# A graph network with product-key memory: edges counted for 32 destinations at a time, and x multiplied by the weights before the aggregation

## The chip, the cores and the metric

The kernel runs on one core of one Trainium2 chip. The metric is the device time of one execution in microseconds (us), the median of several runs.

## The reference, cut to what matters

x is 1250 x 512, float32. The graph has 21,250 edges (10,000 random pairs in both directions and 1250 loops), sorted by destination. Four stages follow each other, each added to x:

```python
x = x + L0_gnn(layernorm(x))    # the stage that the change touches
x = x + L0_ffn(layernorm(x))    # 8 heads, top 8 of 256 x 256 keys, two 512-wide rows gathered for each hit
x = x + L1_gnn(layernorm(x))    # aggregation over the same edges
x = x + L1_ffn(layernorm(x))    # one of 8 experts for each row
```

Stage L0_gnn, written out:

```python
xw = x @ W.T
row, col = concat(src, loop), concat(dst, loop)
dinv = rsqrt(segment_sum(1, col))
out = segment_sum(dinv[row] * dinv[col] * xw[row], col) + b
h = (out - mean(out)) * rsqrt(var(out) + eps) * gamma + beta   # mean, var over the 1250 rows
return gelu(h) + x
```

## The kernel before

The rows are padded to 1280, which is NT = 10 tiles of 128. The core first builds the dense table of edge counts AT[source, destination] (1280 x 1280, float32) and uses it for both aggregations.

Counting (`pe_program`, L1573 to L1602; `act_program`, L679 to L710; `dve_program`, L986 to L1029). The edge list is loaded as NS = 84 rows of 256 edges and transposed, so that 128 edges lie on the partitions. For each tile t of 128 destinations the registers hold which edge rows touch it (`pairs_of`, L645: one load from SBUF and two register results), and a loop runs over them. A step takes four blocks of 128 edges. VectorE writes for each block a 128 x 1280 fp16 table of marks (L996) that says which source each edge has; ScalarE writes a 128 x 128 fp16 table that says which destination (L681, L689); TensorE multiplies the two and adds up in PSUM (L1580, 1280 columns for a block). ScalarE copies a finished tile of counts to AT (`keep_counts`, L695). Between tiles VectorE adds up columns (L1008, L1010), TensorE finishes the sums (L1570, in-degrees), and VectorE takes the row statistics of x (L933).

Aggregation. VectorE makes the degree roots and scaled rows h0 (L1045 to L1055), and TensorE multiplies h0 with AT (`piece`, L1608: 4 feature blocks, 10 source tiles, three ranges of 512, 512 and 226 destinations). VectorE scales by the destinations' roots (L1086) and TensorE multiplies with the weights (L1657: 4 output blocks, 4 feature blocks, the same three ranges). Beside it one reduction over all of AT gives the out-degrees (L1073), the residual is formed (L1080), loops are taken off AT (L1093), and ScalarE turns AT into int16 for the second graph stage (L740).

Batch norm and gelu, for each block o of 128 features (`out_row` and `gelu`, L744 to L760, and L1107 to L1117): ScalarE adds the bias, VectorE takes statistics, ScalarE a square root, VectorE the scale and shift, ScalarE the gelu. Square root and gelu need different activation tables, each with its own load.

Then comes the memory stage (L763 on): searches, indirect gathers of 2 x 512 numbers by GpSimd (L587, each 128 rows), dot products on VectorE (L1313), a diagonal on ScalarE (L883) and a product on TensorE (L1786). It begins with the first tile whose four feature blocks have had their gelu. The last stages are L1714, L1861 and L1883.

The order on each engine is the order of the program; each engine waits for counters of the others. SP issues the loads in this order: edges, x, first weights, parameters, query weights, keys, and 34 writes that clear a scratch table in HBM.

## Time and profile before

| what | value |
|---|---|
| runs | 1264.42, 1264.74, 1264.78 us; median 1264.74 |
| profiled execution, first to last instruction (span) | 1262.0 us; 2.7 us lie around it when set against the median of the runs |
| TensorE, VectorE, ScalarE, GpSimd busy | 91%, 73%, 41%, 51% of the span |
| counting | 14.9 to 134 us |
| aggregation | 134 to 222 us |
| product with the first weights | 222 to 256 us |
| memory stage | from 260 us; first gather issued at 284.9 us |

The profile names engines PE (TensorE), PEld (its weight loads), DVE (VectorE), ACT (ScalarE), POOL (GpSimd) and SP; a q behind a name is the engine's sequencer, which does register work, waits and branches. A float32 matmul shows as two records.

### The profile page before, as it was taken

How to read it: one execution, taken by the hardware profiler on the slowest of the kernel's cores; microseconds unless marked ns; L12 is line 12 of the kernel's file. 1: busy time of each engine (PE TensorE's matmuls, PEld its weight loads, DVE VectorE, ACT ScalarE, POOL GpSimd, SP SyncE). 2: the span in 40 equal slices, each digit the busy share in tenths (PEclk: the TensorE clock that was granted, in tenths of full speed). 3: DMA queues.
4: the chain of work that ended last, by engine and by line, in shares of the span. 5: the costliest groups of instructions: out<-in, count | busy, mean ns of one | idle time of the engine just before them, and what ended most of it. 6: DMA issues, size and time to landing. Idle time of an engine off the chain costs nothing.

```text
span 1262.0 us, 15214 instructions
## 1 busy us (share of the span) xinstructions
PE 1145.0 (91%) x3900; PEld 572.9 (45%) x3901; DVE 925.5 (73%) x2783; ACT 514.7 (41%) x1254; POOL 640.5 (51%) x698
## 2 busy tenths in 40 slices
PE   5999999965999998899998998989989889989497
PEld 2555555553444444354444444534444344334243
DVE  6999831357899987978879789788797877665311
ACT  7889103642435343443444434443444333320010
POOL 1000000007667777777777776777767776631322
PEclk9999999986999999999999999999999999989699
DMA  8999000008989999999999999999999999944643
GB/s 336 418 421 418 29 0 1 1 0 345 383 353 388 409 409 408 409 409 410 409 409 408 410 409 408 409 410 408 409 409 397 410 408 381 410 174 163 234 139 109
DMA packets 107763, 406.07 MB, mean 322 GB/s; under 512 B 11946, under 2 KB 12112, under 8 KB 103332
## 3 DMA queue, kind: packets, MB, share of 16 engines
q0 software_dynamic: 92992, 337.10, 67.6%
q1 hardware_dynamic: 14692, 68.07, 13.8%
q8 instruction: 30, 0.49, 0.2%
q14 instruction: 49, 0.40, 0.1%
HBM read 353.24 MB, written 53.00 MB: 322 GB/s over the span
## 4 chain that ended last, share of the span: by engine, by line
PE 53%; DVE 14%; DMA 13%; POOL 9%; issue 5%; ACT 2%; DVEq 2%; ACTq 0%; SPq 0%; POOLq 0%
PE tr L1786 19%; PE acc L1580 8%; DMA big<-in_wdu,idx 7%; PE acc L1608 7%; POOL big L587 6%; PE acc L1714 4%; DMA AT<-in_wdu,idx 4%; DVE big L1313 4%; PE acc L1687 3%; PE tr L1883 3%; PE acc L1657 3%; POOL AT L587 3%; PE tr L1861 2%; PE acc L1698 2%; DVE AT L1313 2%
## 5 line engine op out<-in xcount | busy, mean ns | idle before, releaser
L587 POOL DMA_INDIRECT big<-in_wdu,idx x460 | 434.2, 944 | 435.3 <-DVE idx L1377 279.3
L1786 PE MATMUL tr<-big,diag 128*128 128x512 f32 x920 | 427.1, 602 | 31.8 <-ACT diag L883 31.2
L1313 DVE CUSTOM_DVE_ANT_0 big<-big,acc,prob 128x512 f32<-128x512 f32 x460 | 322.9, 742 | 68.2 <-DMA big<-in_wdu,idx 66.7
L883 ACT ACTIVATE diag<-ident,inner 128x128 f32<-128x128 f32 x576 | 199.3, 393 | 414.2 <-DVE inner L1313 412.3
L1786 PEld LDWEIGHTS tr<-big,diag 128*128 128x128 f32 x920 | 166.9, 190 | 249.0 <-issue 167.1
L587 POOL DMA_INDIRECT AT<-in_wdu,idx x168 | 163.6, 974 | 61.8 <-issue 46.0
L1786 PE MATMUL tr<-AT,diag 128*128 128x512 f32 x336 | 157.0, 600 | 8.7 <-ACT diag L883 8.7
L1313 DVE CUSTOM_DVE_ANT_0 AT<-AT,acc,prob 128x512 f32<-128x512 f32 x168 | 118.0, 743 | 25.2 <-DMA AT<-in_wdu,idx 24.2
L1580 PE MATMUL acc<-outT,diag 128*128 128x512 f16 (+1 forms) x600 | 112.7, 349 | 4.0 <-ACT diag L689 3.8
L996 DVE TENSOR_SCALAR outT<-big 128x1280 f16<-128x1280 f16 x200 | 96.6, 547 | 6.1 <-PE acc L1580 3.2
L1786 PEld LDWEIGHTS tr<-AT,diag 128*128 128x128 f32 x336 | 61.0, 190 | 86.2 <-issue 62.1
L1687 PEld LDWEIGHTS acc<-yT,qk 128*128 128x128 f32 x640 | 79.9, 199 | 18.7 <-issue 16.6
L1608 PE MATMUL acc<-AT,big 128*128 128x512 f32 (+1 forms) x240 | 84.6, 513 | 0.0
L1580 PEld LDWEIGHTS acc<-outT,diag 128*128 128x128 f16 x600 | 59.1, 100 | 54.5 <-ACT diag L689 3.5
L1687 PE MATMUL acc<-yT,qk 128*128 128x128 f32 x640 | 82.5, 284 | 1.4 <-ACT yT L777 1.4
L1714 PE MATMUL acc<-wide,h1bc 128*128 128x512 f32 (+1 forms) x144 | 60.9, 518 | 3.6 <-issue 3.6
L1608 PEld LDWEIGHTS acc<-AT,big 128*128 128x128 f32 x240 | 45.4, 190 | 37.9 <-issue 37.8
L681 ACT ACTIVATE gt<-big 128x128 f16<-128x128 f16 x200 | 61.4, 387 | 2.1 <-issue 2.0
L1313 DVE DVE_READ_ACCUMULATOR2_ANT inner<- 128x1 f32 x628 | 51.8, 82 | 0.0
L1698 PE MATMUL acc<-qk,qT 64*128 64x256 f32 x288 | 50.6, 428 | 0.0
L1714 PE MATMUL acc<-wide,gt 128*128 128x512 f32 (+1 forms) x96 | 43.7, 551 | 6.3 <-ACT wide L830 4.3
L1173 DVE TENSOR_TENSOR outT<-outT,acc 128x512 f32<-128x512 f32 (+1 forms) x60 | 35.0, 585 | 16.8 <-PE acc L1714 16.7
(301 smaller groups left out, 1068.7 us busy)
## 6 DMA issues: line engine op xcount, KB each, us to landing
sorted_rows<-big SPq DMA_DIRECT2D x33, 1280.0 KB, 32.7
big<-in_we SPq DMA_DIRECT2D x8, 1024.0 KB, 14.6
big<-in_wdu,idx POOLq DMA_INDIRECT x460, 10.6
x<-sorted_rows SPq DMA_DIRECT2D x14, 512.5 KB, 3.5
AT<-in_wdu,idx POOLq DMA_INDIRECT x168, 10.8
x<-in_x SPq DMA_DIRECT2D x1, 2304.0 KB
qk<-in_wq SPq DMA_DIRECT2D x1, 2048.0 KB, 15.4
big<-in_w0t SPq DMA_DIRECT2D x1, 1024.0 KB, 12.3
```

The lines of the kernel that those rows point to most:

```text
L587: pool.indirect_dma_start(out=k.slot[r * GS + s], out_offset=None, in_=k.wdu_d, in_offset=bass.IndirectOffsetOnAxis(ap=k.idx[i % 2][:, j:j ...
L681: ins = act.activation(k.far[:, (half * BPS + b) * P:(half * BPS + b + 1) * P], k.iota[:, NPAD + t * P:NPAD + (t + 1) * P], ACT.Abs, bias= ...
L883: ins = act.activation(k.diag[:, c * P:(c + 1) * P], to, ACT.Relu, scale=k.inner[:, j:j + 1])
L996: ins = dve.tensor_scalar(k.ohs[:, (half * BPS + c) * NPAD:(half * BPS + c + 1) * NPAD], k.iota[:, t * P:t * P + NPAD], k.key[:, bass.ds(c ...
L1313: ins = dve.tensor_tensor_reduce(out=row, in0=row, in1=k.Y[i % 2] if i < NT - 1 else k.Yh[j // WIDTH], scale=k.prob[:, (i % 2) * HK + j:(i ...
L1580: ins = pe.matmul(acc[:, c0:c0 + n], k.ohb[:, (half * BPS + b) * P:(half * BPS + b + 1) * P], k.ohs[:, (half * BPS + b) * NPAD + c0:(half ...
L1608: return pe.matmul(k.acc[s][:, c0:c0 + n], k.h0[:, t * D + f * P:t * D + (f + 1) * P], k.AT[:, t * NPAD + c0:t * NPAD + c0 + n], start=(t ...
L1657: ins = pe.matmul(k.acc[o % 2][:, c0:c0 + n], k.w0[:, f * D + o * P:f * D + (o + 1) * P], k.aggT[:, f * NPAD + c0:f * NPAD + c0 + n], star ...
L1687: ins = pe.matmul(k.Q[:, (h % 4) * P:(h % 4 + 1) * P], k.wq[:, f * H * P + h * P:f * H * P + (h + 1) * P], k.yT[:, f * P:(f + 1) * P], sta ...
L1698: ins = pe.matmul(k.S[:, c, 0:NK], k.qT[half, (h % 4) * P:(h % 4 + 1) * P], k.keys[half, h * NK:(h + 1) * NK], start=True, stop=True)
L1714: ins = pe.matmul(k.G[n % 2 if n >= TWO_BANKS else 0][:, 0:cols], k.h1[j % 3][:, f * P:(f + 1) * P], k.wide[:, at:at + cols], start=(j == ...
L1786: ins = pe.matmul(k.O[i % 2], k.diag[:, c:c + P], row, start=(g == 0 and s == 0), stop=(g == groups_of(i) - 1 and s == GS - 1))
```

## The change

The change replaces the stage L0_gnn and its preparation:

- Counting goes by windows of WIN = 32 destinations, NW = 40 in all. An edge block's stationary operand is a 128 x 128 fp16 table: source modulo 128. The moving operand is 320 marks: 10 source tiles times 32 destinations. The stationary tables of all 168 blocks are made once, before the loop, by `one_hots`; the marks are made in the windows by `marks`. Each window takes FIXED = 2 edge rows in straight code, with two sets of buffers, and the rest (at least one) in a loop with one buffer. Columns are chosen by a register.
- In-degrees come from a histogram of small products before the windows (destination modulo 32 times destination divided by 32), not from sums over AT.
- TensorE multiplies x, loaded once more in transposed form, by the first weights before the aggregation. The layer norm's mean is taken out of the weights (W less its mean over the features, by GpSimd), and its scale goes onto the product (`keep_xw`).
- The aggregation multiplies the result with AT, by range of destinations: 12 parts, of which eight run between windows (`PART_AFTER`) and four, of 226 destinations, after the last. VectorE scales a part, ScalarE adds the bias.
- The diagonal of roots, the loops in AT and the int16 table go to GpSimd. The out-degree reduction stands in two halves around the first of the last four parts, ahead of the batch norm of block 0; the residual lies between the batch norms.
- SP loads w0 and x transposed ahead of x, clears the scratch table in 68 writes, and loads query weights and keys after the last window.

```diff
-SPAN = BPS // 2 * P
+SPAN = 2 * P
+WIN = 32
+NW = NPAD // WIN
+CODES = NT * WIN
+FIXED = 2
+PARTS = [(c0, n, o) for c0, n in SPANS for o in range(FT)]
+PART_AFTER = {17: 0, 20: 1, 23: 2, 26: 3, 33: 4, 35: 5, 37: 6, 39: 7}
+TILES_OF = [4, 8, NT]
 def pool_program(pool, k):
...
+    pool.wait_ge(k.wmean_ready, 1)
+    for f in range(FT):
+        rows = k.w0[:, f * D:(f + 1) * D]
+        pool.tensor_tensor(rows, rows, k.wmean, ALU.subtract)
+    pool.drain().then_inc(k.wc_ready, 1)
...
+    for t in range(NT):
+        pool.wait_ge(k.at_done, (t + 1) * (P // WIN))
+        pool.tensor_tensor(loops(t), loops(t), k.ident[:, :], ALU.add).then_inc(k.loops_done, 1)
+    pool.wait_ge(k.sums_done, 1)
+    for t in range(NT):
...
+        pool.tensor_tensor(loops(t), loops(t), k.ident[:, :], ALU.subtract)
+        pool.drain()
+        pool.tensor_copy(k.few[:, t * NPAD:(t + 1) * NPAD] if t else k.few0, k.AT[:, t * NPAD:(t + 1) * NPAD])
 def act_program(act, k):
...
+    keep_xw(0)
+    for w in range(NW + 2):
+        if w < NW:
+            keep_counts(w)
+        for t in kept_after.get(w, []):
+            keep_xw(t)
...
+        if w - 2 in PART_AFTER:
+            biased(PART_AFTER[w - 2])
 def dve_program(dve, k):
...
+    def one_hots(out, codes, n, block):
+        cols = slice(block * BLOCK, (block + 1) * BLOCK)
+        return dve.tensor_tensor(out[:, 0:n, cols], codes[:, cols].unsqueeze(1).to_broadcast([P, n, BLOCK]),
+                                 k.iotaX[:, 0:n, :], ALU.is_equal)
+    for block in range(4):
+        one_hots(k.lo_hot, k.lo16, WIN, block)
+        one_hots(k.hi_hot, k.hi16, NW, block)
+        dve.drain().then_inc(k.hist_ready, 1)
...
+    for block in range(4):
+        one_hots(k.table, k.src16, P, block)
...
+    def marks(w, first):
+        end, shift = rows_of(dve, k, w)
+        base = column(dve, k, (first + shift) * 2, 2 * (NS - 1))
+        for row in range(FIXED):
+            if w >= 2 and row == 0:
+                dve.wait_ge(k.fixed_used, w - 1)
+            for c in range(2):
+                ins = dve.tensor_scalar(k.fixed[w % 2][2 * row + c], k.iota,
+                                        k.key[:, 2 * row + c:KEYS][:, bass.ds(base, 1)], -float(CODES * w),
+                                        ALU.subtract, ALU.is_equal)
+            ins.then_inc(k.fixed_ready, 1)
+        with dve.Fori(first, end) as row:
+            col = column(dve, k, (row + shift) * 2, 2 * (NS - 1))
+            dve.wait_ge(k.looped_used, row + 1)
...
+            ins.then_inc(k.looped_ready, 1)
+    first = marks(0, 0)
+    dve.wait_ge(k.indeg_psum, 1)
...
+        stats(k.x[:, t * D:(t + 1) * D], t)
...
+    first = marks(1, first)
...
+    dve.drain().then_inc(k.coef_ready, 1)
+    for w in range(2, NW + 4):
+        if w < NW:
+            first = marks(w, first)
+        if w - 2 in PART_AFTER:
+            scaled_part(PART_AFTER[w - 2])
+        if w - 4 in PART_AFTER:
+            part_stats(PART_AFTER[w - 4])
...
+    out_degrees(0, NT // 2)
+    scaled_part(EARLY)
+    out_degrees(NT // 2, NT)
+    dve.drain().then_inc(k.sums_done, 1)
...
+    norm_row(0)
+    scaled_part(EARLY + 1)
+    for t in range(NT // 2):
+        residual(t)
+    norm_row(1)
+    scaled_part(EARLY + 2)
+    for t in range(NT // 2, NT):
+        residual(t)
...
+    norm_row(2)
+    scaled_part(EARLY + 3)
+    norm_row(3)
 def pe_program(pe, k):
...
+    def window(w, first):
+        end, shift = rows_of(pe, k, w)
+        base = column(pe, k, (first + shift) * 2, 2 * (NS - 1))
+        if w >= 2:
+            pe.wait_ge(k.at_done, w - 1)
+        for row in range(FIXED):
+            pe.wait_ge(k.fixed_ready, FIXED * w + row + 1)
+            for c in range(2):
+                ins = chunk(w, base, 2 * row + c, k.fixed[w % 2][2 * row + c], row == 0 and c == 0)
+        ins.then_inc(k.fixed_used, 1)
+        with pe.Fori(first, end) as row:
...
+            pe.wait_ge(k.looped_ready, row + 1)
+            for c in range(2):
+                ins = chunk(w, col, 2 * FIXED + c, k.looped[c], False)
+            ins.then_inc(k.looped_used, 1)
...
+    weighted(0)
+    pe.wait_ge(k.bounds_ready, 1)
...
+    histogram()
+    weighted(1)
+    weighted(2)
+    in_degrees()
+    weighted(3)
+    pe.wait_ge(k.table_ready, 1)
+    first = 0
+    for w in range(NW):
+        first = window(w, first)
+        if w + 4 < NT:
+            weighted(w + 4)
...
+        if w in PART_AFTER:
+            part(PART_AFTER[w])
+    for p in range(EARLY, len(PARTS)):
+        part(p)
```

## Rows read from the trace of the kernel before

**Rows 1.** The page: its span and the busy time of each engine.

```profile
span 1262.0 us, 15214 instructions
PE 1145.0 (91%) x3900; PEld 572.9 (45%) x3901; DVE 925.5 (73%) x2783; ACT 514.7 (41%) x1254; POOL 640.5 (51%) x698
```

**Rows 2.** Busy time in stretches: PE, PEld, DVE, ACT, POOL, clock, DMA share, GB/s.

```profile
30.00:110.00 80.00, 79.58 (x475) 45.01 (x473) 77.52 (x158) 71.30 (x180) 0.00 (x0) 1.00 1.01 419
160.00:210.00 50.00, 50.00 (x144) 27.17 (x143) 11.22 (x20) 4.02 (x4) 0.00 (x0) 1.00 0.00 0
300.00:1100.00 800.00, 750.39 (x2368) 360.67 (x2369) 664.90 (x2138) 331.01 (x869) 585.62 (x617) 0.99 1.02 403
```

**Rows 3.** The chain that ended last, in order of time: start, length, what.

```profile
4.37 0.42 DVE big L937
14.89 13.77 PE acc L1580 x60
51.77 10.84 PE acc L1580 x60
159.47 62.95 PE acc L1608 x180
222.42 33.21 PE acc L1657 x94
259.60 2.01 ACT outT L756 x3
```

**Rows 4.** The first gather, in the timeline of GpSimd.

```profile
284.88 1.21 POOL L587 DMA_INDIRECT big<-in_wdu,idx  x1 [279.28 <-DVE idx L1377]
```

**Rows 5.** Groups by shape, 0 to 262 us: shapes and count, busy, mean ns, idle before.

```profile
L681 ACT ACTIVATE gt<-big 128x128 f16<-128x128 f16 x200 | 61.4, 387 | 2.1 <-issue 2.0
L1073 DVE TENSOR_REDUCE degin<-AT 128x10 f32<-128x12800 f32 x1 | 13.5, 13487 | 0.1
L933 DVE BATCH_NORM_STATS2 st<-x 128x6 f32<-128x512 f32 x10 | 6.8, 685 | 0.0
L1080 DVE TENSOR_SCALAR x<-x,pq 128x512 f32<-128x512 f32 x10 | 4.7, 545 | 0.1
L747 ACT ACTIVATE outT<-acc,par 128x226 f32<-128x226 f32 x4 | 1.8, 443 | 0.0
```

**Rows 6.** The same list, by shape, 262 to 1262 us, and of GpSimd.

```profile
L1224 DVE TENSOR_TENSOR pick<-pick,topf 128x1024 f16<-128x1024 f16 x9 | 6.2, 692 | 0.8
L607 POOL TENSOR_TENSOR x<-x,qk 128x512 f32<-128x512 f32 x10 | 12.3, 1279 | 0.3 <-issue 0.3
```

**Rows 7.** VectorE's timeline in the counting: start, length, what.

```profile
13.11 3.79 DVE L996 TENSOR_SCALAR outT<-big 128x1280 f16<-128x1280 f16 x8 [1.36 <-issue]
```

**Rows 8.** The sequencers' records at L647, L996 and L1022: ns min/median/max.

```profile
L647 DVEq TENSOR_LOAD <-bnd x10: 306/570/646, 11.9 to 107.6; - x10
L647 DVEq FUSED_REGOPS  x10: 190/211/212, 12.5 to 108.2; - x10
L996 DVEq FUSED_REGOPS  x200: 57/57/202, 13.0 to 129.8; - x100
L1022 DVEq COMPARE_BRANCH  x20: 50/56/80, 19.8 to 130.1; - x20
```

**Rows 9.** Small matmuls in the timeline, 118 to 162 us.

```profile
120.14 0.23 PEld L1602 LDWEIGHTS acc<-big 128*128 128x128 f16 x3
```

**Rows 10.** The end of the stage before, in the timeline of 222 to 262 us.

```profile
239.91 1.28 ACT L750 ACT_TABLE_LOAD   x1
241.20 0.29 ACT L750 ACTIVATE bsd<-bmv,eps 128x1 f32<-128x1 f32 x1
241.51 1.28 ACT L756 ACT_TABLE_LOAD   x1
242.81 1.46 ACT L756 ACTIVATE outT<-outT,bsc 128x1280 f32<-128x1280 f32 x1
```

**Rows 11.** Busy time in stretches, as in rows 2: in the start of the memory stage.

```profile
290.00:300.00 10.00, 2.52 (x12) 1.79 (x11) 8.00 (x32) 1.54 (x2) 7.72 (x8) 0.50 0.97 364
```

718 lines of the change are left out of this document (326 added, 392 removed).

## The prediction

> **What bounds the kernel now.** Read the page's busy times first, then stretches, then the chain of waits. TensorE is busy 91% of the span [rows 1], but for different reasons: while it counts and aggregates it never rests (79.6 of 80 us, 50.0 of 50, [rows 2]); in the memory stage (300 to 1100 us) it is busy too, but there the DMA share is 1.02 at 403 GB/s, and the change touches neither. The chain is one TensorE line after another until the last product with the weights ends at 255.6 us, and the batch norm's last block starts its gelu at 259.6 [rows 3]; the first gather follows at 284.9 [rows 4]. So the question is only when that gelu starts; everything later moves with it, one for one. The profiled execution spans 1262.0 us and the median of the runs is 1264.7, so I work out differences and take them from 1264.7.
>
> **What TensorE saves.** Before, 60 matmuls of the counting, which are 20 blocks of 1280 columns in three pieces each, take 10.84 us [rows 3]: 0.54 us a block, 0.42 ns a column. I ran the reference's input formula for the graph: with rows of 256 edges the 40 windows touch 2 to 4 rows each, and with 2 fixed and at least 1 looped row they run 124 rows, 248 blocks (four windows, 11, 19, 25 and 31, loop twice). At 320 columns that is 248 x 320 x 0.42 = 33.6 us, 0.14 a block, 0.85 a window with one loop; before it was 119 us. The float32 products stay: 180 records in 62.95 us [rows 3] are 90 matmuls, 30 each of 512, 512 and 226 columns, 1.68 ns a column, so 0.86 us for 512 columns. A tile of x times weights is 4 of these, 3.44 us, ten are 34.4 (before 33.2); a part of 512 destinations is 10, 8.6 us, eight are 69; a part of 226 is 3.8, four are 15. New: a histogram of 168 pairs (weight load, product). Three fp16 pairs of one column take 0.23 us [rows 9], so 0.075 each and 12.6 us; half and double that (6 to 25) are its ends. TensorE alone would be some 55 us shorter. What follows says how much of it waits.
>
> **Before the windows.** VectorE starts at 4.4 as before [rows 3]. Codes, flags and bounds are ops of 0.4 us like L937's; I take 10 us for the start of the one-hots. An fp16 tensor_tensor of 1024 elements takes 0.69 us [rows 6]: 0.53 for elements at two a cycle, 0.16 fixed. A histogram block (1408 and 1760 elements) is 2.0 us, four 8.0; bounds 1.7; four table blocks of 5632 elements 3.1 each, 12.3: done at 32. (At one element a cycle the blocks would be done at 50, and the windows 5 later.) TensorE: flips until 11, four sums over w0 3.4, ScalarE's mean 0.7, four subtractions on GpSimd at 1.23 (ten of them in 12.3, [rows 6]) to 20.3, tile 0 to 23.9, histogram to 36.6, tiles 1 and 2 to 43.5, in-degrees to 44.5, tile 3: window 0 begins at 48. Its end is at 49, but then tile 4 needs a bank freed by `keep_xw`, which waits for coef_ready. That chain is on VectorE: degrees 0.5 after 44.5, ten statistics of x 6.2 to 6.9 [rows 5], their aggregation 0.9, marks of window 1 (2.3, below), roots 0.8, ScalarE's copy 0.7: 56. TensorE idles 7 us behind it; everything in its queue, tiles and windows, is behind that wait.
>
> **Windows.** VectorE's mark op of 1280 fp16 elements repeats every 0.474 us (8 in 3.79, [rows 7]): four elements a cycle leave 0.33, so 0.14 is fixed and 320 elements cost 0.22. Six are 1.3 us. The sequencer needs more: the load of the window's word 0.31 to 0.57, two register results 0.21, the base column about 0.2, 0.06 for each mark's address, branches 0.06 each [rows 8]; with 0.07 to issue an op that is 2.2. Before, this work hid behind marks of 0.47; now the loop's wait for `looped_used` lets little overlap. I take 2.3 us a window where VectorE sets the pace; ends 1.7 (all register work hidden but one load) and 3.2 (nothing overlaps, and the round trip to TensorE, about 0.7, is added). Where TensorE has other work VectorE runs up to 1.7 windows ahead and a window costs TensorE its 0.85 to 1.
> - Tiles 4 to 9 beside windows 1 to 5: 6 x 3.44 + 5 x 0.95 = 25.4, from 56 to 81.5, and 1.7 for a slow clock after the idle time: at 25% busy the granted clock was 0.50, 1.2 GHz [rows 11]. 83.
> - Windows 6 to 17: 12 x 2.3 = 27.6, and 1.5 for the spread of roots: 112.
> - Eight parts, 68.8, in which nothing counts. Windows between them: after a part the first costs 0.85, the second 1, the third 2.6 with the scaling in VectorE's queue (0.7, taken like the statistics of 512 columns, [rows 5]): three triples 13.5; windows 27 to 33 4.5 + 4 x 2.3 = 13.7; three pairs 5.7. Second loops 2.8, slow clock at parts 0 and 4 3.4. Part 7 ends at 112 + 107.9 = 220.
> ScalarE's copies of counts (320 columns; 128 cost 0.39, [rows 5]) take about 0.6 a window and hide. GpSimd's loops and roots hide too: forty windows lie over them. The scratch table's writes are over long before the gathers, at 400 GB/s for 44 MB.
>
> **The tail grows.** Before, the four parts of the last 34 us came 8.3 us apart, and a block's norm (6 us) fitted under the next one's product; only 4 us stood behind TensorE. Now four parts end 3.8 us apart, but the norms queue. After part 7: scaling, bias, statistics 2.4; half of the out-degrees 6.7 (the whole is 13.5 for 12,800 elements, [rows 5]), scaling of part 8 0.5, the other half 6.7: 16.3. Then block 0: statistics, aggregation, root, table load, gelu. One block costs table 1.28, root 0.3, table 1.28, gelu 1.46 [rows 10] and 0.44 of bias; the residual (five of 0.5, L1080 in [rows 5]) stands before the statistics of blocks 1 and 2. Block 0's gelu ends at 20.5, block 1's at 26.4 (its table is loaded by the degree root before it), block 2's at 31.8, and block 3's starts at 35.1. TensorE's own last part ended at 15: 20 us of tail stand open against 4 before.
>
> **Sum.** 220 + 35.1 = 255.1 against 259.6: 4.5 us earlier. GpSimd's int16 copies of AT can start at 16.3 after part 7 and have until the first gather, 25.3 after the gelu, thus 44 us for ten steps and an eleventh copy. A subtraction of 128 columns is about 0.3, the drains 0.4, a copy of 1280 between 1.3 (an element a ns) and 3.1 (L607's 2.4 ns an element): 22 to 42 us. It fits, barely at the upper end. Query weights (3 MB, some 8 us after window 39) land long before. Forecast 1264.7 - 4.5 = 1260.2, say 1260. By its own terms this case holds 1253 to 1266: half the histogram's price is -6, 0.3 on 20 VectorE-bound windows is +6.
>
> **Rivals.**
> A. The windows are cheap: at 1.7 instead of 2.3 us 20 windows give 12 back: 1248. For it: register loads are hidden before (idle before L996 for issue is a single 1.36 at the start, [rows 7]). Against: the ops that hid them were twice as long.
> B, slower. The hand-over between VectorE and TensorE decides: each window has a load on both sequencers and one single looped buffer, so marks, signal, product and signal stand in a row. From 2.55 us a window on it eats the gain (4.5 over 20 windows is 0.22); at 3.1 it costs 16 more: 1276. For it: sequencer work of over 1 us a window is in rows 8. Against: only one row a window uses the single buffer, and the next window's fixed marks can be written meanwhile.
> C, slower. GpSimd's subtraction, which TensorE waits for before tile 0, is held by VectorE's one-hots. If each of the last two of its four operations waits for a table block of 3.1 us, window 0 begins 7 us later: 1267. No row shows the two engines so; ten operations of GpSimd beside VectorE's sums out of PSUM kept 1.23 us [rows 6]. The Trainium skill, SBUF — State Buffer, section "SBUF: two separate sides", says that VectorE (with two SBUF inputs) and a GpSimd operation reading SBUF take a shared port pair exclusively for a whole instruction; by that rule C comes true, and otherwise not.
> D. The marks with two arithmetic steps run at one element a cycle: 0.25 more each, 1.5 a window: 1290.
> E. GpSimd's copies are late and hold the first gather: each us over 4 a copy costs 11; at 4.5, 1266.
>
> **Chances.** Forecast 0.42 (of it faster 0.30, no change 0.08, slower 0.04), A 0.18, B 0.19, C 0.13 (0.02 of it no change), D 0.03, E 0.05 (0.03 no change). A measurement tells about 0.2%, 2.5 us, from no change. Faster: 0.30 + 0.18 = 0.48, and 0.04 more where B and C are partly made good by A: 0.52. No change 0.13, slower 0.35. The range reaches from A's 1248 to most of B: 1247 to 1275; the forecast's own is 1253 to 1266.
>
> **What would show it.** Window 0 at about 48 us, tile 4 at 56; a mark of about 0.2 us; VectorE-bound windows every 2.3 us with TensorE under half busy; part 7 ending near 220; the last gelu's start 35 us behind it. If parts and tail are right and the windows differ, the sum fails in the 2.3. If the tail is under 30 or the gathers don't follow 25 us after the gelu, the chain that I wrote down isn't the one that binds. Forecast is wrong outside 1253 to 1266.

## The result, and the profile after

| what | value |
|---|---|
| kernel before | 1264.76 us median (1264.42 to 1265.6, 4 runs) |
| changed kernel | 1291.96 us median (1291.04 to 1292.48, 4 runs) |
| ratio | 1.0215, 95% interval [1.0200, 1.0229]: slower by 27.2 us |
| predicted | 1260.0 us (1247 to 1275), faster: wrong, and on the wrong side |

The page of the changed kernel, as in [rows 1]:

```profile
span 1289.1 us, 14872 instructions
PE 1121.7 (87%) x3670; PEld 567.4 (44%) x3671; DVE 896.2 (70%) x2788; ACT 420.0 (33%) x1029; POOL 681.9 (53%) x754
```

TensorE, VectorE and ScalarE all do less work than before, and the kernel is slower: the time is idle time and a lower clock, not work. The stretches (columns as in [rows 2]) are windows 6 to 17, the eight parts with windows 18 to 39, and the memory stage:

```profile
96.20:129.50 33.30, 22.13 (x102) 14.21 (x100) 16.20 (x68) 7.22 (x16) 1.39 (x3) 0.59 1.01 404
129.50:245.60 116.10, 102.87 (x324) 52.79 (x323) 40.50 (x149) 14.34 (x30) 2.80 (x6) 0.91 0.08 29
300.00:1100.00 800.00, 739.48 (x2383) 359.42 (x2384) 669.74 (x2179) 327.57 (x856) 580.41 (x607) 0.99 1.00 395
```

In windows 6 to 17 (first line) TensorE is busy 22 of 33 us, and that at a granted clock of 0.59, between its two levels 0.50 (1.2 GHz) and 1.00 (2.4 GHz); VectorE, which I had as the engine that sets the pace, is busy only 16. The memory stage (last line) moves its bytes nearly as before. The chain that ended last, in order of time:

```profile
16.60 6.50 POOLq L618
23.14 5.79 PE acc L1619 x8
29.17 16.92 PE tr L1629 x168
46.09 9.66 PE acc L1619 x16
...
58.43 4.75 DVE st L977 x8
68.19 5.45 PE acc L1619 x8
...
127.71 1.82 PE acc L1642 x6
129.54 10.57 PE acc L1679 x20
...
236.85 8.71 PE acc L1679 x20
247.89 6.68 DVE degout L1115
254.86 6.73 DVE degout L1115
...
284.91 2.01 ACT outT L797 x3
```

From top to bottom: GpSimd's subtractions, tile 0, the histogram, tiles 1 and 2, (cut) VectorE's statistics of x, tile 4, (cut) window 17, part 0, (cut) part 7, the two halves of the out-degrees, and (cut) the gelu of block 3. That gelu began at 259.60 before [rows 3]: it is 25.3 us later, and the kernel 27.2. The first gather follows 26.0 behind it, as it did before (25.3, [rows 4]):

```profile
310.86 1.21 POOL L657 DMA_INDIRECT big<-in_wdu,idx  x1 [27.91 <-DVE idx L1416]
```

So the frame of the prediction held: what counts is when that gelu starts. The four stages before it, each against what the prediction has:

| stage | predicted us | measured us | late by |
|---|---|---|---|
| start, to the end of window 5 | 0 to 83 | 0 to 96.2 | 13.2 |
| windows 6 to 17, and spreading the roots | 29 | 33.3 | 4.3 |
| eight parts and windows 18 to 39 | 107.9 | 116.1 | 8.2 |
| tail, part 7's end to block 3's gelu | 35.1 | 39.3 | 4.2 |

Together 29.9, and 1.9 more come behind the gelu; 1260.2 + 31.8 is the measured time.

### The profile page after: what moved, and what is told of

Read it like the earlier page. It is cut to its first block, busy times and chain, and to the rows that moved or that the text cites. A ratio compares the mean times of both kernels' runs of the same rounds, so it can differ in the third digit from the quotient of the medians.

```text
span 1289.1 us, 14872 instructions
## 1 busy us (share of the span) xinstructions
PE 1121.7 (87%) x3670; PEld 567.4 (44%) x3671; DVE 896.2 (70%) x2788; ACT 420.0 (33%) x1029; POOL 681.9 (53%) x754
## 4 chain that ended last, share of the span: by engine, by line
PE 47%; DVE 18%; DMA 13%; POOL 9%; issue 7%; DVEq 3%; ACT 2%; POOLq 1%; SPq 0%; ACTq 0%
PE tr L1835 18%; DMA big<-in_wdu,idx 7%; PE acc L1679 6%; POOL big L657 6%; DVE big L1352 4%; PE acc L1763 4%; DMA AT<-in_wdu,idx 4%; PE acc L1736 3%; PE acc L1642 3%; POOL AT L657 3%; PE acc L1619 3%; PE tr L1932 3%; PE tr L1910 2%; DVE AT L1352 2%; PE acc L1747 2%
## 5 line engine op out<-in xcount | busy, mean ns | idle before, releaser
L1835 PE MATMUL tr<-big,back 128*128 128x512 f32 x920 | 428.7, 603 | 31.7 <-ACT back L927 30.9
L927 ACT ACTIVATE back<-ident,inner 128x128 f32<-128x128 f32 x576 | 199.3, 394 | 414.2 <-DVE inner L1352 412.3
L1835 PEld LDWEIGHTS tr<-big,back 128*128 128x128 f32 x920 | 167.0, 190 | 250.4 <-issue 167.7
L1835 PE MATMUL tr<-AT,back 128*128 128x512 f32 x336 | 157.0, 600 | 8.0 <-ACT back L927 7.9
L1763 PE MATMUL acc<-front 128*128 128x512 f32 (+1 forms) x240 | 98.8, 532 | 10.4 <-issue 6.0
L1835 PEld LDWEIGHTS tr<-AT,back 128*128 128x128 f32 x336 | 61.1, 190 | 85.4 <-issue 61.6
L1736 PEld LDWEIGHTS acc<-front 128*128 128x128 f32 x640 | 79.9, 199 | 18.7 <-issue 16.6
L1736 PE MATMUL acc<-front 128*128 128x128 f32 x640 | 82.7, 284 | 1.4 <-ACT front L821 1.4
L1065 DVE TENSOR_SCALAR back<-big 128x320 f16<-128x320 f16 x88 | 23.0, 302 | 73.0 <-PE acc L1642 72.5
L1763 PEld LDWEIGHTS acc<-front 128*128 128x128 f32 x240 | 44.5, 194 | 62.0 <-issue 56.9
L1057 DVE TENSOR_SCALAR back<-big 128x320 f16<-128x320 f16 x160 | 38.6, 304 | 33.8 <-issue 26.9
L1222 DVE FIND_INDEX8 topi<-top,back 128x8 uint32<-128x256 f32 x144 | 58.5, 419 | 0.0
```

Of the source, the lines that this page charges most:

```text
L927: ins = act.activation(k.diag[:, c * P:(c + 1) * P], to, ACT.Relu, scale=k.inner[:, j:j + 1])
L1222: ins = dve.max_index(k.topi[:, c * HK + h * 8:c * HK + h * 8 + 8], k.top[:, c * HK + h * 8:c * HK + h * 8 + 8], k.sc[h % 2][:, c * NK:(c ...
L1736: ins = pe.matmul(k.Q[:, (h % 4) * P:(h % 4 + 1) * P], k.wq[:, f * H * P + h * P:f * H * P + (h + 1) * P], k.yT[:, f * P:(f + 1) * P], sta ...
L1763: ins = pe.matmul(k.G[n % 2 if n >= TWO_BANKS else 0][:, 0:cols], k.h1[j % 3][:, f * P:(f + 1) * P], k.wide[:, at:at + cols], start=(j == ...
L1835: ins = pe.matmul(k.O[i % 2], k.diag[:, c:c + P], row, start=(g == 0 and s == 0), stop=(g == groups_of(i) - 1 and s == GS - 1))
```

## Experiments

Where nothing else is said, a kernel is the changed one with only the edit shown. "Gelu" is the start of block 3's gelu in its trace (259.6 before, 284.9 in the changed kernel). The kernel before, run beside each group, took 1264.3 to 1264.9 us, with one exception told at e9.

One thing has to be known for reading "gelu". Tile 0 begins at 23.0 to 23.5 us in some traces (the changed kernel, e6, e9, e10, e12, e13, e16) and at 26.3 in others (e1, e3, e4, e5, e14, e17), though nothing in front of it was edited; why is told at rival C. So gelus of two traces compare within 3 us only. Lengths of single stretches don't have this error.

**e1_stats_early.** The statistics of x before VectorE's wait for the histogram.

```diff
+    (statistics of x and their aggregation)
     dve.wait_ge(k.hist_psum, 1)
...
     dve.drain().then_inc(k.degs_ready, 1)
-    (statistics of x and their aggregation)
```

> The row statistics of x and their aggregation (7.1 us on VectorE from 57 to 64 us, on the way to the scale that tile 4 of x times weights waits for) are moved ahead of the copy of the histogram, where VectorE stood idle for 10.5 us. Theory 1, the preparation sets the start and everything behind it is delayed one for one: tile 4 starts some 6 to 7 us earlier (at about 62 instead of 68.2), the total falls by as much, to about 1285.5. Rival, the windows' own pace absorbs it (the first windows become bound by marks): less than 3 us.

Measured 1286.32 us (1284.14 to 1286.97), ratio 1.0168 [1.0151, 1.0185]: 5.6 less than the changed kernel. Tile 4 began at 65.8 in place of 68.2 although tile 0 began 3.2 later in this trace (26.3, against 23.1): the wait was real. From tile 0 to the end of tile 9 this trace needs 64.9 us, the changed kernel 72.3, 7.4 less, a little more than the 6 to 7 of theory 1. Where the statistics stand is worth 5 us or more.

**e2_hist_first.** TensorE's histogram in the place where it waited for GpSimd.

```diff
-    weighted(0)
+    histogram()
     pe.wait_ge(k.bounds_ready, 1)
...
-    histogram()
+    weighted(0)
     weighted(1)
```

> TensorE's order only: the 168 small products of the histogram stand ahead of tile 0, in the 7.2 us that TensorE idled until GpSimd had taken the mean off the weights. Theory 1: window 0 and tile 4 come about 6 us earlier, total about 1286. Rival, the small products run at the lower clock there and tiles 0 to 3 then too, or the histogram waits for its marks of VectorE until 20.8 us: 2 to 4 us, total about 1289.

Measured 1282.45 us (1280.65 to 1283.73), ratio 1.0141: 9.5 less, more than both theories had. The chain of this kernel has no GpSimd in it any more; the sums over w0 are followed at once by the histogram, and that by three tiles:

```profile
11.06 5.62 PE acc L1608 x8
16.69 16.92 PE tr L1629 x168
...
33.96 13.10 PE acc L1619 x24
```

The histogram keeps its 16.9 us. The granted clock over it is 0.66 here and 0.65 in the changed kernel, although here TensorE was busy without a break before it and in it: the clock fell over these small products without any wait. The idle 7 us before tile 0 are gone, and so is some of the slow clock behind them: tiles 0 to 2 take 13.1 here, 15.5 in the changed kernel (5.79 and 9.66).

**e3_outdeg_split.** The out-degrees range by range between the windows, only the last range in the tail.

```diff
     for w in range(2, NW + 4):
...
+        if w == 22: degrees_of(0)    # 10 x 512 columns
+        if w == 37: degrees_of(1)
...
-    out_degrees(0, NT // 2)
-    scaled_part(EARLY)
-    out_degrees(NT // 2, NT)
+    degrees_of(2)                    # 10 x 256 columns
+    scaled_part(EARLY)
+    (two sums of 128 x 10)
```

> The out-degree reduction (13.5 us in two halves behind part 7, ahead of block 0's batch norm) is done by ranges of destinations: the first 512 and the second 512 in VectorE's idle time beside parts, 256 at the end. Theory 2, the tail is one chain behind part 7 and the reduction stands in it: the 13.5 become 2.7 and two small additions, the last gelu starts 10 us earlier, total about 1282. Rival, the chain of table loads and batch norms behind the last parts (15 us from part 7 to the end of part 11) takes over: part 8 to 11 end 3.8 us apart and a block needs 4.9, so 7 to 8 us, total about 1284.5. If it gave nothing, the tail is not what binds.

Measured 1285.25 us (1283.64 to 1286.07), ratio 1.0162: 6.7 less. The tail itself fell from 39.3 to 27.8 us, more than either theory had; the rest was lost before it. The first of the two stood one or two windows too late in VectorE's order. VectorE's timeline in this kernel:

```profile
157.93 0.52 DVE L1065 TENSOR_SCALAR back<-big 128x320 f16<-128x320 f16 x2 [6.79 <-PE acc L1651]
158.66 5.49 DVE L1109 TENSOR_REDUCE degout<-AT 128x10 f32<-128x5120 f32 x1 [0.22 <-issue]
```

The marks of a looped row wait 6.8 us for TensorE, which is busy with a part; only then does the reduction start, when TensorE needs marks again. Part 2 began 7.3 us later than in the changed kernel (of which part 0 already had 1.9), and so part of the gain was paid back. An operation meant to hide under a part must stand ahead of the marks that wait for that part.

**e4_static.** The rows of each window as constants in the code: no word loaded, no register column, no loop; same buffers, waits and order. It holds for this graph alone.

```diff
-    word = eng.value_load(k.bnd[0:1, w:w + 1], ...)
-    return eng.snap(word >> 12), eng.snap((word & (END - 1)) - SHIFT)
+    first = sum(LOOPED[:w])
+    return first + LOOPED[w], LOWS[w] - first
...
-        with dve.Fori(first, end) as row:
+        for row in range(first, end):
```

> The rows that each window takes are constants of this graph: no register loads, no address work, no loop; the marks, products, buffers and waits are the same. Theory 3, register work on VectorE's and TensorE's sequencers sets the pace (theory of the prediction, 2.3 us a window of which 1.3 is marks): windows 8 to 17 fall from 2.6 us to about 1.5, the total by about 20, to 1272. Rival, the hand-over over the single buffer of the looped row (signal, marks 0.5, signal, two products, signal): windows stay above 2.2 us and the total falls by less than 8. Second rival, TensorE at 1.2 GHz sets it (six products take 1.82 us instead of 0.83): windows stay at about 2.2.

Measured 1263.22 us (1259.73 to 1265.45, 10 runs), ratio 0.9983 [0.9972, 0.9994]: 28.7 less, as much as the whole loss against the kernel before (27.2). That doesn't make it the only thing that costs: e1, e2 and e3 find their gains elsewhere. The clock is full from 100 us to the end of part 7,

```profile
100.00:120.00 20.00, 17.14 (x91) 10.32 (x90) 15.53 (x68) 6.07 (x14) 1.58 (x3) 1.00 1.02 406
120.00:160.00 40.00, 36.79 (x128) 18.92 (x128) 16.56 (x64) 5.78 (x12) 1.08 (x2) 1.00 0.26 103
```

and windows that nothing else disturbs come 1.27 us apart, which is VectorE's six marks.

**e5_fill.** Is the clock the cause or the consequence? Two fp16 products of 512 columns that nothing reads, behind each of windows 9 to 33 that no part follows.

```diff
+        if 8 < w < 34 and w not in PART_AFTER:
+            for _ in range(2):
+                pe.matmul(k.tr[1], k.zero[:, 0:P], (512 columns), start=True, stop=True)
```

> Two products of 512 fp16 columns that nothing reads stand behind each window from 9 to 33 that has no part behind it; they take TensorE 0.43 us at 2.4 GHz, 0.86 at 1.2. Everything else is the changed kernel. Theory, the low clock (granted 0.50 from 100 to 120 us) sets the pace of the windows: the clock stays at 2.4 GHz, windows fall from 2.6 to about 2.1 us, parts 0, 2 and 4 lose their slow start (1.8 us each), the total falls by 10 or more, to about 1281. Rival, register work sets it and the low clock is only what follows from TensorE's waiting: the clock rises but windows stay at 2.4 to 2.6, and only the slow starts go: 3 to 6 us, total about 1287. If the filler stands in the way, the total rises.

Measured 1287.07 us (1284.7 to 1288.57), ratio 1.0168: 4.9 less.

```profile
120.00:160.00 40.00, 34.37 (x126) 17.54 (x124) 15.97 (x63) 5.60 (x12) 0.99 (x2) 0.96 0.27 105
```

```profile
122.12 1.25 PE L1642 MATMUL acc<-back,front 128*128 128x320 f16 x6 [0.79 <-ACT AT L752]
...
123.32 0.59 PE L1664 MATMUL tr<-front,big 128*128 128x512 f16 x2
124.77 1.22 PE L1642 MATMUL acc<-back,front 128*128 128x320 f16 x6 [0.85 <-ACT AT L752]
```

The first row is the stretch, the others TensorE's timeline; the third is the two added products. The granted clock is up (0.96, against 0.83 over 120 to 160 us in the changed kernel; 1.00 over 118 to 124, against 0.50 over 118 to 123), and the windows still come 2.6 us apart, with 0.8 us in which TensorE does nothing. One might object that the added products eat what the clock gives (0.59 us here, and six products took 1.82 and now 1.22). The records of TensorE's sequencer rule that out. The load of the window's word starts at 120.7 and 123.3 here, while the added products still run, and at 118.5 and 121.1 in the changed kernel: 2.6 us both times, 1.4 from the load to the first of the six products and 1.2 to issue the six. The low clock does not make the pace, the sequencer does. The parts gained, since fewer of them start slow: part 0 takes 8.8 us, 10.6 in the changed kernel.

**e6_ahead.** Each window's word is loaded one window ahead, before the loop, on both engines.

```diff
     def marks(w, first, rows):
         end, shift = rows
...
+        if w + 1 < NW:
+            rows = rows_of(dve, k, w + 1)
         with dve.Fori(first, end) as row:
```

> The general kernel with its loops, but each window's word is loaded and taken apart (0.31 + 0.20 us on VectorE's sequencer, 0.31 + 0.16 on TensorE's) before the loop of the window in front, where the sequencers wait for each other anyway. Theory, the register work stands on the chain of the window (the 28.7 us that the constants gave back are mostly loads and results of loads): 0.5 us a window in 14 windows bound by it, 6 to 10 us in all, total about 1284. Rival, it is the loop itself (its column register, the two branches, the end) that the constants took away: under 3 us.

Measured 1292.61 us (1291.72 to 1293.43): no gain. The latency of the load is not what is waited for. The records of the sequencers say why: they work one instruction after another, and the load takes its time of a sequencer wherever it stands (VectorE's and TensorE's in the changed kernel, ns min/median/max):

```profile
L717 DVEq TENSOR_LOAD <-big x40: 299/312/820, 46.4 to 227.1; - x40
L717 DVEq FUSED_REGOPS  x40: 190/204/205, 47.3 to 227.5; - x40
...
L1057 DVEq FUSED_REGOPS  x160: 57/64/202, 47.7 to 228.5; - x160
...
L1061 DVEq COMPARE_BRANCH  x44: 43/43/67, 49.3 to 235.8; - x44
...
L717 PEldq TENSOR_LOAD <-big x40: 295/306/771, 55.7 to 229.7; - x40
L717 PEldq FUSED_REGOPS  x40: 156/157/165, 56.5 to 230.1; - x40
...
L1642 PEldq FUSED_REGOPS  x248: 46/52/146, 57.0 to 236.3; - x124
```

All such records of a window, summed with the medians, are 1.29 us on VectorE and 1.10 on TensorE. The medians hide two levels of the load. Here are the loads of the changed kernel from 98 to 127 us, then from 131 to 245:

```profile
L717 PEldq TENSOR_LOAD <-big x10: 489/556/630, 100.5 to 126.4; - x10
L717 DVEq TENSOR_LOAD <-big x9: 546/569/586, 99.5 to 124.9; - x9
```

```profile
L717 PEldq TENSOR_LOAD <-big x22: 295/300/308, 131.3 to 229.7; - x22
L717 DVEq TENSOR_LOAD <-big x20: 299/304/315, 142.9 to 227.1; - x20
```

Up to 127 us the writes of the scratch table run (408 GB/s over 100 to 127); behind them a load takes half as long. The step lies at 126 to 131 us in e5, e12, e13 and e17 too, whichever window is due then. No run moved the writes, so that they are the reason is argued, not shown. In windows 6 to 17 the sums are thus about 1.55 us on VectorE and 1.35 on TensorE.

**e9, e10, e14: load and columns, or loop?** In e9 the loops' lengths are constants and the loops straight code; the word is loaded and every column is a register. In e10 the loops stay, with constants for their ends and for the first row; the looped row's column comes out of a register only where a loop runs twice (the trace shows 8 column results in place of 88).

```diff
 e9:
-    return eng.snap(word >> 12), eng.snap((word & (END - 1)) - SHIFT)
+    return sum(LOOPED[:w + 1]), eng.snap((word & (END - 1)) - SHIFT)
-        with dve.Fori(first, end) as row:
+        for row in range(first, end):
 e10:
-    word = eng.value_load(...)
-    return eng.snap(word >> 12), eng.snap((word & (END - 1)) - SHIFT)
+    first = sum(LOOPED[:w])
+    return first + LOOPED[w], LOWS[w] - first
         with dve.Fori(first, end) as row:
```

> The changed kernel, but each window's number of looped rows stands in the code, so the step that was in a loop is straight code; each window's word is still loaded into a register on both engines, and every column still comes from a register. Constants for everything gave 28.7 us back, loading the word a window ahead gave nothing. Theory: the loop itself (its branch, the register work and waits inside it that nothing can be moved past) makes a window 2.6 us; then this run keeps at least 20 of the 28.7 us: 1265 to 1272, windows 6 to 17 at 1.3 to 1.8 us. Rival: the load and the register columns are the cost (six columns computed for each engine in each window), the loop only adds its branch of 0.06 us; then it gains under 8: 1284 to 1291, windows 2.3 us or more.

> The counterpart: loops stay loops (one pass, in four windows two), but their ends, and the columns of the two fixed rows, are constants; no word is loaded; only the looped row's column is computed from the loop's counter. If the loop itself is the cost, this stays near the changed kernel: 1280 to 1290, windows 6 to 17 at 2.2 to 2.6 us. If the load and the fixed rows' register columns are, it comes close to constants for everything: 1264 to 1270. If each has its own share, the two runs lie about half way each, near 1277.

> The kernel with loops and constants once more, on a chip where the kernel before takes 1264 and not 1367 us. In its first trace block 3's gelu began at 253.8 us, 31 earlier than in the changed kernel and 5.8 earlier than before. If the later stages follow one for one, it takes 1259 (1256 to 1262); if loops with constants delay something that only the later stages show, it stays at 1264 to 1267, as the first ratio (1.0019) had it.

These (and e11, e15) ran in two sessions in which every kernel took 100 us longer: the kernel before had 1366.73 and 1369.9 us there. The traces of e9 to e11 move 357 GB/s over 300 to 1100 us, e14's 360, in place of 403; up to the gelu they look like the others. They bear the chip number of e1 to e4, so what differed is not known. e9 took 1379.97, ratio 1.0088 [1.0058, 1.0118]; e10 1369.37, ratio 1.0019 [0.9995, 1.0043]; e14, the same kernel, 1366.85, ratio 1.0003 [0.9978, 1.0028]. The question of e14, and of e15 below, how fast the kernel is where the one before takes 1264 us, stayed open. The changed kernel was not timed in them, so I compare the starts of the gelu: 269.1 in e9, 253.8 and 257.1 in e10 and e14 (tile 0 begins 2.8 us later in e14), 256.2 in e4. VectorE in e10:

```profile
108.49 0.51 DVE L1070 TENSOR_SCALAR back<-big 128x320 f16<-128x320 f16 x2
108.91 0.93 DVE L1062 TENSOR_SCALAR back<-big 128x320 f16<-128x320 f16 x4
```

and in the changed kernel, in the same stage:

```profile
108.65 0.94 DVE L1057 TENSOR_SCALAR back<-big 128x320 f16<-128x320 f16 x4 [1.55 <-PE acc L1642]
109.50 0.51 DVE L1065 TENSOR_SCALAR back<-big 128x320 f16<-128x320 f16 x2
111.80 0.52 DVE L1065 TENSOR_SCALAR back<-big 128x320 f16<-128x320 f16 x2 [1.78 <-PE acc L1642]
```

The theory stated for both (the loop itself is the cost) fell: with loops and branches but nothing to load and almost nothing to work out, marks stand back to back as in straight code. e9 gives back 15.8 us at the gelu, about half. The sequencer's register work, with the medians, is about 0.17 us a window in e10, 1.04 in e9 and 1.29 in the changed kernel.

**e12, e13: on which engine?** Constants on VectorE alone, then on TensorE alone; the other engine keeps its load, columns and loop.

```diff
 e12: in marks()        e13: the same in window(), with pe
-        end, shift = rows_of(dve, k, w)
-        base = column(dve, k, (first + shift) * 2, 2 * (NS - 1))
+        end, shift = known_rows(w)
+        base = (first + shift) * 2
-        with dve.Fori(first, end) as row:
+        for row in range(first, end):
```

> The changed kernel with constants in place of word, columns and loop on VectorE alone; TensorE keeps its loads, register columns and loop. Theory: VectorE is the late engine, since its register work (1.25 us a window by the summed records) and its six marks (1.3 us) add up to the 2.6 us that a window takes; then this run comes near constants on both, block 3's gelu starting 22 to 29 us earlier than in the changed kernel (256 to 263 us). Rival: TensorE's own register work between six products holds it (gap of 0.8 us behind each six); then it gains under 12 us, and the next run has the larger part.

> The counterpart: constants on TensorE alone; VectorE keeps its loads, register columns and loop. If VectorE is the late engine, this gains 0 to 8 us: block 3's gelu at 277 to 285 us. If TensorE is, it has 20 us or more. If both stand in one chain (marks, signal, products, signal, with the register work of each in it), each run gains about half, 10 to 18 us, and the two add up to what constants on both gave.

Measured e12 1284.16 us (1282.22 to 1285.56), ratio 1.0150 [1.0129, 1.0171], gelu 280.5; e13 1283.47 us (1282.11 to 1286.32), ratio 1.0147 [1.0123, 1.0171], gelu 275.8. For e12 the rival came true: under 12 us, and e13 has the larger part at the gelu (9.1, against 4.4). None of the three theories stated for e13 has its result. Neither engine alone gives much, and the two gains, 7.8 and 8.5, are 16 of e4's 28.7. The timeline of TensorE in e12, then the chain in e12 and in e13, windows 16 and 17 and the start of part 0:

```profile
113.89 1.82 PE L1651 MATMUL acc<-back,front 128*128 128x320 f16 x6 [1.20 <-DVE back L1066]
...
116.67 1.82 PE L1651 MATMUL acc<-back,front 128*128 128x320 f16 x6 [0.95 <-ACT AT L761]
```

```profile
124.61 1.82 PE acc L1651 x6
127.24 1.82 PE acc L1651 x6
129.06 10.88 PE acc L1688 x20
```

```profile
124.99 1.80 PE acc L1651 x6
126.79 10.68 PE acc L1688 x20
```

In e12 VectorE is far ahead and waits; TensorE, on its own, needs 2.63 us a window: 1.82 in which it issues six products, and 0.8 of register work in front of them. By e5 this is the sequencer's time and would be the same at full clock. (The releaser in brackets, ScalarE's copy, had ended long before; it is only the last signal that the profile can name.) In e13 TensorE has no register work, and a window takes 2.4: from 112 to 122 us the chain holds nothing but VectorE's loads, results and marks. So the two engines each have a window of 2.4 to 2.6 us, side by side: freeing one leaves the other.

**e16, e17: the amount of register work, or its place behind a wait?** e16 is e13 with VectorE's order changed: the word, columns and fixed marks of window w + 1 before the looped marks of window w, which wait for TensorE. e17 is e9 with two sets of looped buffers used in turn, so that this wait asks for the row before the last.

```diff
 e16:
-    first = marks(w, first)
+    rows.append(fixed_marks(w + 1, rows[w][0]))
+    looped_marks(w, rows[w - 1][0], *rows[w])
 e17:
-    dve.wait_ge(k.looped_used, row + 1)
+    if row >= 2:
+        dve.wait_ge(k.looped_used, row)
     for c in range(2):
-        ins = dve.tensor_scalar(k.looped[c], ...)
+        ins = dve.tensor_scalar(k.looped[row % 2 * 2 + c], ...)
```

> e13 (constants on TensorE) with one change of order on VectorE: the fixed marks of window w + 1, their word and their columns come before the looped marks of window w, which wait for TensorE. Same number of instructions, same buffers. e13 had 30.6 us from the end of tile 9 to the start of part 0, 2.4 a window, and in them VectorE stood 9.7 us waiting for TensorE. If the amount of VectorE's register work (1.3 us a window) beside its marks (1.3 us) sets the pace, nothing changes: 29 to 31 us and 1282 to 1285 in all. If the place of that work is the matter, behind a wait for the single looped buffer, so that the sequencer can't run ahead, it falls to 22 to 27 us, and the whole to 1274 to 1280 (rival B's hand-over, with register work as part of it).

> e9 (loads and register columns on both engines, no loop) with two sets of looped buffers used in turn, so that the marks of a looped row wait for the one before the last. e9 had 27.9 us in that stretch, 2.2 a window. If the hand-over through the single buffer is in the chain, 20 to 25 us; if the amount of register work is, 27 to 28.

e16 took 1289.52 us (1287.97 to 1292.47), ratio 1.0199; e17 1264.88 us (1260.5 to 1267.65), ratio 0.9996 [0.9983, 1.0008]. All traces of this question side by side, in us:

| kernel | end of tile 9 to part 0 | part 0 to end of part 7 | gelu |
|---|---|---|---|
| changed | 34.1 | 116.0 | 284.9 |
| e12, constants on VectorE | 34.1 | 112.2 | 280.5 |
| e13, constants on TensorE | 30.6 | 109.7 | 275.8 |
| e16, e13 with VectorE's order changed | 30.3 | 118.7 | 282.5 |
| e9, registers, no loop | 27.9 | 105.9 | 269.1 |
| e17, e9 with two looped buffers | 25.9 | 97.2 | 260.2 |
| e10, loops with constants | 19.9 | 100.9 | 253.8 |
| e4, constants | 19.6 | 100.1 | 256.2 |

In the first column, where windows follow each other, the order changes nothing (30.3 against 30.6) and the second buffer 2 us, which comes out between its two theories (20 to 25 for the hand-over, 27 to 28 for the amount alone): there it is mostly the amount of register work. In the second column, with parts between the windows, the second buffer is worth 8.7 us: while TensorE does a part, VectorE may write marks for more of the windows that follow it, so that parts 2 and 3 start 12.7 us apart in e17 and 14.0 in e9: the three windows between them take 4.0 in place of 5.3. e17 still loads every word and works out every column, and is 27.1 us faster than the changed kernel. So a loss of this size needed both things together: register work on both engines, and a single buffer and a loop behind which none of it could be done ahead. The single buffer costs a little even alone: between the parts e17 (97.2) is 3 us faster than e4 with its constants (100.1). A kernel with two buffers that keeps its loop was not run. Why e16 lost 9 us between the parts is not settled. Its eight parts took 77.4 us together and e13's 72.6, since four of them ran at a lower clock; that is 5 of the 9. Its fixed marks stand ahead of the looped ones that TensorE needs first when a part ends, which fits, but was not tried apart.

**e7 and e8: do the gains add up?** e7 is general: e1, e2, e3 (its two reductions one window earlier, w = 21 and 36), e6, and the residual between the windows (w = 18 and 24), which takes it out of the tail. e8 has the same moves with e4's constants in place of e6.

> All the moves at once, for any graph: statistics of x ahead of the histogram's copy, histogram ahead of tile 0, out-degrees by ranges and the residual in VectorE's idle time right behind the marks of the window that follows a part (the ranges stood one window too late in the run of the split reduction, where part 2 came 7 us later for it), words loaded a window ahead. By the single runs 5.6 + 9.5 + about 12 + about 6: 1259, which would be faster than the kernel before (1264.9). If the tail's chain of norms binds earlier than counted, or the moves share one gap, 1264 to 1268.

> The same moves with the rows of each window as constants of this graph (no loads, no loops), the floor of this design. Theory, preparation, windows and tail are separate stretches of one chain and their prices add: 1263.2 - 5.6 - 9.5 - 12 = about 1236. Rival, with cheap windows TensorE is busy and the moves find no room: 1245.

e7 took 1260.47 us (1259.24 to 1261.02, 5 runs), ratio 0.9962 [0.9947, 0.9976]: faster than the kernel before by 4.3 us, for any graph. e8 took 1230.68 us (1228.86 to 1231.32), ratio 0.9724 [0.9706, 0.9741]: 34 us faster, for this graph. The prices add up in e7 (1259 expected) and by more than that in e8 (1236). In e7 the gelu begins at 256.3. Its residual, with no GpSimd copies beside it:

```profile
L1115 DVE TENSOR_SCALAR x<-x,pq 128x512 f32<-128x512 f32 x10 | 4.9, 550 | 0.0
```

and in the changed kernel, beside them (both in groups by shape):

```profile
L1119 DVE TENSOR_SCALAR x<-x,pq 128x512 f32<-128x512 f32 x10 | 9.7, 1035 | 0.0
```

**e11, e15 and e18: a faster general version?** e11 and e15 are e7 with e5's products; e18 the same with e16's order in place of e6.

> All four moves that hold for any graph (statistics of x early, histogram first, out-degrees by range between the windows, residual between the windows, word loaded a window ahead: 1260.5 us), and two products of 512 columns that nothing reads behind each of the windows 9 to 33 that no part follows. The fillers alone gave 4.9 us, by raising the granted clock. If that adds to the rest: 1256 (1253 to 1258). If the moves already gave part of it back, or VectorE's longer windows hold the end: 1259 to 1262.

> The general version with all four moves and the filler products once more, on a chip where the kernel before takes 1264 us. Its first trace had block 3's gelu at 249.0 us, 10.6 before that of the kernel before. One for one this is 1254 (1251 to 1257), 6 below the same version without the fillers; if the fillers only move idle time, 1258 to 1262.

> A general version meant to be the fastest: statistics early, histogram first, out-degrees and residual between the windows, unread products behind windows 9 to 33, and VectorE's order of e16. e11, the same without that order and with the word loaded ahead, had 32.5 us from the end of tile 9 to part 0 and block 3's gelu at 249.0 us. With full clock TensorE alone needs 0.83 + 0.8 + 0.5 = 2.1 a window. If VectorE's order is a part of the rest: 27 us there, gelu at 238 to 244, and 8 to 15 us under e11's difference to the kernel before. If not: as e11, ratio 0.995.

e11 and e15 ran in the slower sessions: 1361.26 and 1361.98 us, ratios 0.9962 [0.9935, 0.9989] and 0.9948 [0.9930, 0.9966], gelu at 249.0 both times. e18 took 1260.28 us (1258.85 to 1260.91), ratio 0.9958 [0.9941, 0.9974], gelu at 252.8. The products bring the gelu 7.3 us forward against e7 (256.3), e16's order takes half of that away again, and the time of e18 is no better than e7's. The gain of the products lies in the parts (part 0 to the end of part 7: 118.8 us in e7, 111.2 in e11), not in the windows: from the end of tile 9 to part 0 e7 has 33.7, e11 33.0 and e18 33.1. For e18 27 was expected, from 2.1 us a window at full clock; that is refuted, and again the sequencer holds the window. What e11 takes where the memory stage is not slowed was not measured.

## Why the prediction was wrong

By size, the sum failed first before the windows: 13.2 of the 31.8 us are terms there that were too small. By mechanism it failed in the windows, whose price left TensorE's sequencer out; this step shows in the sum as 4.3 and most of 8.2 us, and a kernel without the register work (e4) gave back 28.7.

**The frame was right.** The gelu of block 3 decides, one for one within 3 us in every trace: e1 +21.0 us at the gelu against the kernel before and +21.5 in time, e2 +16.5 and +17.6, e4 -3.4 and -1.6, e7 -3.3 and -4.3, e12 +20.9 and +19.9, e13 +16.2 and +19.2, e17 +0.6 and 0.0. In the slower sessions it held less well (e10 and e14: -5.8 and -2.5 at the gelu, +2.6 and -3.1 in the medians, where e14's ratio says no change).

**What TensorE saves: right, and beside the point.** 248 products of 320 columns came; their interval at full clock, six in 0.83 us, is the 0.14 I had. "Some 55 us shorter" doesn't follow from the terms given: 85.4 less 12.6 for the histogram, 1.2 for x times weights, 3.4 for the sums over w0 and 1.5 for the roots is 67. It isn't used in the sum. In the traces TensorE's busy time up to the gelu fell by 26 us (241.9 to 215.8), at a granted clock of 0.82 in place of 1.00. It was the idle time and the clock around the products that were mis-sized.

**Before the windows: 13.2 late, by four terms that were too small.** GpSimd's four subtractions took 6.40 us in place of 4.9 (rival C in small, below) and started later, so tile 0 began at 23.1 (not 20.3); tile 0 took 5.8 (not 3.4), behind idle time at a granted clock of 0.63; the histogram 16.9 (not 12.6), 0.10 us a pair where three one-column pairs before [rows 9] had given 0.075; tiles 1 and 2 took 9.7 (not 6.9), at 0.73. These four are 12 us. I priced the slow clock once, at tile 4. It struck behind the wait for GpSimd and in the histogram too, where e2 shows it without a wait in front.

The histogram's ends of 6 to 25 us held its size. What I didn't weigh is that it stood behind a wait that it doesn't need; e2 shows 9.5 us for its place alone.

**Windows: the step that failed is "2.3 us a window where VectorE sets the pace; where TensorE has other work a window costs TensorE its 0.85 to 1".** With TensorE freed of registers e13 runs at 2.4, so VectorE's 2.3 was near (by luck in part: the terms listed for its 2.2 add up to 1.6 to 1.9). TensorE's own price was missing: I had counted the load, the results and the branches on VectorE's sequencer only. TensorE's sequencer needs 1.4 us from its load to the first product and 1.2 more to issue six products with their addresses, 2.63 in all (e12), and that at full clock as at half (e5). The changed kernel runs at 2.6. The 0.83 us that the products need on TensorE never counted.

Rival B had this price (from 2.55 a window the gain is gone) and a load on both sequencers, with the single looped buffer as its mechanism. That is half true. e4 and e10 keep the buffer and all its waits and run their windows at 1.3 us undisturbed, so where windows follow each other the hand-over alone costs nothing; with register work in it, it does, and above all between the parts (e17). I gave B 0.19, on the ground that the next window's marks could be written meanwhile. They could not be written early enough: the sequencer that would work out their columns stands in the wait.

**Parts: 8.2 late.** All at full clock they take 8.69 us, as priced. Parts 0, 2 and 4 took 10.6, 10.4 and 9.8 behind stretches of slow windows (I had 3.4 for slow clock there; it was 4.7); most of the rest is the windows between parts, where e17 shows what the single buffer costs.

**Tail: 39.3, not 35.1.** The order was as written, and the half reductions took 6.8 (6.7 expected). The residual took 4.51 and 5.20 us for five operations where I had 2.5: beside GpSimd's copies one operation costs 1.04 us on average in place of 0.55. The average hides an alternation. An operation that meets one of GpSimd's conversions ends 0.3 us behind it and takes 1.47 us, the next one 0.68:

```profile
266.26 1.36 POOL L639 CAST AT<-AT 128x1280 int16<-128x1280 f32 x1
266.43 1.47 DVE L1119 TENSOR_SCALAR x<-x,pq 128x512 f32<-128x512 f32 x1
```

This is the mirror of rival C, which had VectorE hold GpSimd.

**Rival C itself** is true as a mechanism; only its price depends on the start. In the changed kernel the subtractions took 6.40 us together, 1.63 on average in place of 1.28 [rows 6]:

```profile
L617 POOL TENSOR_TENSOR big<-big,outT 128x512 f32<-128x512 f32 x4 | 6.4, 1628 | 8.4 <-ACT outT L747 8.4
```

One by one they took 1.26, 1.91, 2.09 and 1.26 us. The two long ones met histogram blocks of VectorE, which became longer too: 1.93 and 2.13 us in place of 0.89 and 1.07. The table blocks of 3.1 us began at 23.39, when the last subtraction had ended at 23.04, so in this trace none could hold one. In e1, whose code is the same up to there, the last subtraction begins beside a table block:

```profile
21.29 3.82 DVE L1014 TENSOR_TENSOR front<-big,outT 128x5632 f16<-128x5632 f16 x1
22.12 4.11 POOL L617 TENSOR_TENSOR big<-big,outT 128x512 f32<-128x512 f32 x1
```

It ends at 26.23, 1.1 us behind the block, and takes 4.11 us. So it is in nine of the nineteen traces of changed kernels (e1, e3, e4, e5, e11, e14, e15, e17, e18: 4.10 to 4.14 us). This is what moves tile 0 from 23.1 to 26.3. Rival C had 7 us, for two held operations; one is held, for 3 us. With the histogram first (e2, e7, e8, e11, e15, e18) it hardly matters: tile 0 begins at 33.3 to 34.4 there.

The Trainium skill, SBUF — State Buffer, section "SBUF: two separate sides", has the two take a port pair in turn for whole instructions. The traces agree: whichever of the two starts first runs on, and the other ends 0.8 to 1.1 us behind it, a little less than its own time alone.

**Rivals A, D and E.** A (1.7 us a window) is refuted by 2.6: not the loads' latency counts (e6 moved the loads ahead for nothing), but the sum of register work. D is refuted: marks come 0.22 us apart (four in 0.94 with the last one's whole length). E is refuted: GpSimd's copies took 1.25 us each and were done at 283, before the gelu even began.

**The range.** My own case ended at 1266 and the whole range at 1275. Four stages were each late by 4 to 13 us, and all in the same direction. They share causes: each time TensorE had idled, the granted clock was low in what followed (0.63 at tile 0, 0.83 at part 0), and VectorE and GpSimd held each other both at the start and in the tail. I had added such errors up as if they were free of each other.

## What to carry to other kernels

When work is cut into smaller pieces, count the sequencer's instructions of each piece (loads to registers, column results, branches) on every engine that takes part, next to the time of the piece: here 1.1 to 1.5 us of register work met pieces of 0.8 and 1.3 us, and 85 us less matmul time (119 - 33.6, by the prediction's sum) came out as 27 us more. Give such steps two buffers in straight code, so that a sequencer never stands in a wait with register work behind it. If two engines are both near the pace, relieving one shows little (8 us each here, 28.7 for both); take the work off both before judging. Look at single operations and not at their mean where two engines may hold each other. Put work that depends on nothing (a histogram, row statistics) in front of waits, not behind them, and reductions ahead of the operation that waits for another engine.

## What was not expected of the hardware

- A register load a window ahead gains nothing (1292.61 against 1291.96 us): a sequencer spends its time on it in its turn, wherever it stands. That time was 0.56 us up to 127 us, while the scratch table was written, and 0.30 behind it. A branch costs 0.04 to 0.07 us and, with constants around it, nothing visible (gelu at 253.8 and 257.1 us with loops, 256.2 without).
- TensorE was granted 0.59 over a stretch in which it was busy 22.1 of 33.3 us, with gaps of 0.8 us every 2.6. In e5, with two added products a window, it was busy 23.8 of 33.0 us with gaps as long, and was granted 0.90; the time fell by 4.9 us. The pace of the windows was the same at both clocks.
- fp16 pairs of weight load and product with 40 columns come 0.10 us apart, in the changed kernel as in e2: 168 in 16.92 us each time. The granted clock over them was 0.65 and 0.66, in e2 with no idle time before.
- VectorE and GpSimd held each other for whole operations: a GpSimd subtraction of 1.26 us took 4.11 beside a VectorE block of 3.8, and a VectorE operation with one input (128 x 512 float32) of 0.55 us took 1.47 when it met one of GpSimd's conversions to int16; those kept 1.25 us.
- In two sessions every kernel took 100 us longer, in the stage of indirect gathers (357 to 360 GB/s in place of 403). What differed is not known.
